# Sinkhorn iterations in three chains, mixing by small diagonals, and Pool's long steps in four pieces

## The reference, cut to what matters

```python
x_norm = x * rsqrt(mean(x * x) + eps)             # x is the normalised sum, 4 streams of C = 256
H_res  = sinkhorn(x_norm @ W_res.T + base)        # 4x4, 50 iterations of row and column normalisation
H_pre, H_post = softmax(x_norm @ W_pre.T + ...), softmax(x_norm @ W_post.T + ...)
H_res  = (1 - g) * I + g * H_res
y      = sum_n(x[n] * H_pre[n]) @ W_branch        # 256
out[i] = sum_j(H_res[i, j] * x[j]) + y * H_post[i]
```

## Time and profile before

| | |
|---|---|
| median of 3 runs | 1298.62 us (1297.89 to 1299.15) |
| the profiled execution | 1296.82 us |
| its span, first to last instruction | 1295.0 us |
| granted clock of PE, mean | 0.916 of 2.4 GHz |
| busy PE, DVE, ACT, POOL | 1070.1, 989.8, 616.4, 546.5 us |
| start of the mixing phase | 1100 us |

### The profile page before, as it was taken

The page is one execution under the profiler, slowest core; times in us unless marked ns, Lnnn a source line. Parts: engine busy times, 40 slices in busy tenths (PEclk is TensorE's granted clock), DMA queues, the critical chain, the costliest instruction groups (busy, mean ns, idle before and its releaser), DMA issues. The chain is left out here.

```text
span 1295.0 us, 24193 instructions
## 1 busy us (share of the span) xinstructions
PE 1070.1 (83%) x8048; PEld 826.3 (64%) x8048; DVE 989.8 (76%) x2908; ACT 616.4 (48%) x1758; POOL 546.5 (42%) x678
## 2 busy tenths in 40 slices
PE   5699999999999999996479999998788874096182
PEld 4477777777877777775356677776566543085071
DVE  6766677766666677765158777787999898999998
ACT  6444455555444455555156776776455542311110
POOL 2523344333333444333137665665454340153194
PEclk9799999999999999998789999999998885597596
DMA  8011101111111101111222232232122111622012
GB/s 362 23 56 40 54 18 55 55 55 55 55 53 41 48 23 55 56 40 40 100 87 76 87 122 85 75 117 86 65 75 70 37 57 41 245 74 89 16 66 97
DMA packets 28652, 95.43 MB, mean 74 GB/s; under 512 B 3760, under 2 KB 7856, under 8 KB 28592
## 3 DMA queue, kind: packets, MB, share of 16 engines
q1 hardware_dynamic: 28592, 94.69, 20.0%
HBM read 64.27 MB, written 27.26 MB: 71 GB/s over the span
## 5 line engine op out<-in xcount | busy, mean ns | idle before, releaser
L614 POOL TENSOR_TENSOR prob_G<-prob_G,rl 128x512 f32<-128x512 f32 x96 | 100.0, 1042 | 258.1 <-DVE rl L502 258.1
L384 ACT ACTIVATE prob_G<-prob_G,negm 128x128 f32<-128x128 f32 x384 | 148.8, 388 | 89.6 <-DVE negm L444 89.6
L245 PE MATMUL ps_qkv<-w_hi,xT_hi 128*128 128x512 f32 x384 | 156.2, 407 | 13.5 <-DVE prob_G L507 8.5
L246 PE MATMUL ps_qkv<-w_lo,xT_hi 128*128 128x512 f32 x384 | 151.4, 394 | 0.0
L247 PE MATMUL ps_qkv<-w_hi,xT_lo 128*128 128x512 f32 x384 | 150.9, 393 | 0.0
L317 PE MATMUL ps_qkv<-wo_hi,aT_hi 128*128 128x512 f32 x256 | 108.0, 422 | 0.0
L319 PE MATMUL ps_qkv<-wo_hi,aT_lo 128*128 128x512 f32 x256 | 102.3, 399 | 0.0
L318 PE MATMUL ps_qkv<-wo_lo,aT_hi 128*128 128x512 f32 x256 | 102.1, 399 | 0.0
L245 PEld LDWEIGHTS ps_qkv<-w_hi,xT_hi 128*128 128x128 f32 x384 | 73.0, 190 | 39.4 <-issue 16.5
L1482 PE MATMUL p_out<-m_xr,m_diag 128*128 128x256 f32 x240 | 58.1, 409 | 46.9 <-POOL m_diag L1649 37.0
L440 DVE TENSOR_TENSOR prob_G<-ps_s,mask 128x512 f32<-128x512 f32 x96 | 65.0, 677 | 41.6 <-PE ps_s L228 41.1
(11 more groups left out here) (218 smaller groups left out, 2987.7 us busy)
## 6 DMA issues: line engine op xcount, KB each, us to landing
rows<-c_row SPq DMA_DIRECT2D x16, 640.0 KB, 3.3
xin<-in_x SPq DMA_DIRECT2D x16, 512.0 KB, 3.3
xres<-in_x SPq DMA_DIRECT2D x16, 512.0 KB, 5.3
x<-xres SPq DMA_DIRECT2D x16, 512.0 KB, 2.6
c_xin<-x SPq DMA_DIRECT2D x16, 512.0 KB, 5.0
c_cin<-in_ctx SPq DMA_DIRECT2D x16, 512.0 KB, 4.3
c_b_xres<-x SPq DMA_DIRECT2D x16, 512.0 KB, 3.2
m_late_row<-rows SPq DMA_DIRECT2D x10, 640.0 KB, 10.9
```

The costliest lines, as they stand in the source:

```text
L245: nc.tensor.matmul(ps_qkv[:, n, :], xT_hi[:, k, :], w_hi[:, k, cols], start=k == 0, stop=False)
L246: nc.tensor.matmul(ps_qkv[:, n, :], xT_hi[:, k, :], w_lo[:, k, cols], start=False, stop=False)
L384: r = nc.scalar.activation(prob(g)[:, j, :], prob(g)[:, j, :], ACT.Exp, bias=negm[:, h:h + 1], accum_out=lsum[:, h:h + 1])
L614: nc.gpsimd.tensor_tensor(prob(g), prob(g), rl[:, g * GROUP:(g + 1) * GROUP].rearrange("p (j o) -> p j o", o=1).to_broadcast([P, GROUP, T] ...
```

## The change: what it does

- **Chains.** There are three, `a` of 5 sequences, `b` of 8, `c` of 3 (`ROWS_OF_CHAINS`). Chain a runs wholly in rounds 6 to 15, 40 steps in each of the rounds 8 to 14, and has more places to be put: behind each product, each pick of weights and each `tq`. Chain b starts in round 14 and has 126 of its steps behind it when the mixing phase begins, c 16. There `weave` lets them take turns, with a few steps of one alone where the other waits for a logarithm; the last steps of c are alone. All is written out, with no loop.
- **Rows.** `rows_x` keeps the normalised features with the lanes regrouped (32 tokens of each of four streams on 128 lanes), `rows_y` the branch. SP issues five DMAs for a row where it issued one.
- **Mixing.** A sequence takes four matmuls over 128 rows and four over 32 rows, 256 columns each, with diagonals of 128x640 in one step: POOL makes them for a and b, DVE for c. For this the coefficients are spread over the lanes: four small matmuls a chain (`sel`), and copies by ACT (for c two by DVE). ACT brings results out in quarters of 256 columns (for c half of them DVE). DVE no longer mixes. The output goes out in four DMAs a sequence.
- **ACT's order** in the mixing phase: copies of a, sequences 0 and 1, the logarithms of b's first block, sequences 2 to 4, those of c's first block and of b's second, copies of b, sequences 5 to 11, the last logarithms of c, sequence 12, copies of c, the last three.
- **POOL's long steps.** From b = 6 the splits (of the sequence two ahead) and the sums run in four pieces of 256 columns. The division of the weights isn't split.
- **Weights.** In rounds 1 to 7 PE transposes them right behind the query's transform rather than behind the key's, and ACT copies them before the key's spectrum.
- The looped rounds are 3 and 4; before they were 3 to 6.

```diff
+ROWS_OF_CHAINS = (5, 8, 3)
+LOOPED = 4
+def weave(dve, *targets):
+    while any(chain.issued < to for chain, to in targets):
+        for chain, to in targets:
+            advance(dve, chain, to, 1)
...
+        for b in range(8, B - 1):
+            if b == 11:
+                parts = {0: at + 3, 1: at + 9, 2: END[0], 3: END[1], 4: END[1] + 10}
+            else:
+                parts = {0: at + 3, 1: at + 9, 2: at + 29, 4: at + 40}
...
+        steps_to[14, 0] += ((one_b, 2),)
+        steps_to[14, 2] += ((one_b, 3),)
+        steps_to[14, 4] += ((one_b, 6),)
+        steps_to.update({(15, 0): ((one_b, 8), (one_a, END[2])), (15, 1): ((one_b, 22),), (15, 2): ((one_a, END[3]), (one_b, 46)), (15, 3): ((one_b, 50),),
+                         (15, 4): ((one_b, 56),), (16, 0): ((one_b, 88),), (16, 3): ((one_c, 2),), (16, 4): ((one_b, 100), (one_c, 6)),
+                         (17, 0): ((one_b, 116),), (17, 4): ((one_b, 126), (one_c, 16))})
+        logs_at = {(6, 1): ((one_a, 1),), (6, 2): ((one_a, 2),), (7, 0): ((one_a, 3),), (7, 1): ((one_a, 4),), (7, 2): ((one_a, 5),),
+                   (11, 2): ((one_a, 6), (one_a, 7), (one_a, 8)),
+                   (14, 1): ((one_b, 1),), (14, 2): ((one_b, 2),), (15, 0): ((one_b, 3), (one_b, 4), (one_b, 5)),
+                   (15, 1): ((one_a, 9), (one_a, 10)), (15, 2): ((one_a, 11),),
+                   (16, 2): ((one_c, 1), (one_c, 2)), (17, 2): ((one_c, 3), (one_c, 4), (one_c, 5))}
...
                     split3(p_a, 0, xn_hi, xn_lo).then_inc(q_ps, 1)
+                    if far and weights_first(b):
+                        transpose_weights()
...
+                chain_logs(b, 0)
+                if far and weights_first(b):
+                    weights_out()
                 if near:
                     key_spectrum(0, f_b)
                     key_spectrum(1, f_c)
...
+            def in_parts(b, dst, a, of, op):
+                width = C if isinstance(b, int) and b >= 6 else D
+                for at in range(0, D, width):
+                    cols = slice(at, at + width)
+                    r = TT(dst[:, cols], a[:, cols], of[:, cols], op)
+                return r
...
+            for chain in chains:
+                pe.wait_ge(coef_step, COEFS * (group(chain) + 1))
+                for g in range(NS):
+                    r = nc.tensor.matmul(p_sel[:, g, 0:chain.n * OWN], sel_sb[:, g, :],
+                                         coef[:, rows, :].rearrange("p b k -> p (b k)"), start=True, stop=True)
+                pe.wait_ge(rows_in[group(chain)], 32 * chain.n)
+                for n in range(chain.first_row, chain.first_row + chain.n):
+                    for g in range(NS):
+                        if 0 < n <= LAST:
+                            pe.wait_ge(out_done, NS * (n - 1) + g + 1)
+                        nc.tensor.matmul(p_out[:, g, 0:C], d[:, g * NS:(g + 1) * NS, :].rearrange("p i t -> p (i t)"),
+                                         xm[n][:, g, :], start=True, stop=False)
+                    for g in range(NS):
+                        lanes = slice(g * W, (g + 1) * W)
+                        nc.tensor.matmul(p_out[:, g, 0:C], d[lanes, N2:N2 + NS, :].rearrange("p i t -> p (i t)"),
+                                         ym[n][lanes, :], start=False, stop=True).then_inc(mix_ps, 1)
...
+            copies(one_a)
+            take_out(0, 2)
+            logs(one_b, FIRST_LOGS + 1, FIRST_LOGS + BLOCK_LOGS)
+            take_out(2, one_a.n)
+            logs(one_c, FIRST_LOGS + 1, FIRST_LOGS + BLOCK_LOGS)
+            logs(one_b, FIRST_LOGS + BLOCK_LOGS + 1, FIRST_LOGS + 2 * BLOCK_LOGS)
+            copies(one_b)
+            take_out(one_b.first_row, LAST - 1)
+            logs(one_c, FIRST_LOGS + BLOCK_LOGS + 1, FIRST_LOGS + 2 * BLOCK_LOGS)
+            take_out(LAST - 1, LAST)
+            copies(one_c)
+            take_out(LAST, B)
```

More of the change, by code:

```diff
@@ L849, in autocorrelation_phase @@
[L849 to L860, removed]
@@ L1095, in body @@
                     key_spectrum(1, f_c)
-                if far:
-                    act.wait_ge(wT_ps, b + 1)
-                    for n in range(2):
-                        nc.scalar.activation(wT[:, n * HALF:(n + 1) * HALF], p_d[:, n, :], ACT.Copy).then_inc(wT_done, 1)
+                if far and not weights_first(b):
+                    weights_out()
                 if ahead:
@@ L1355, in _, with mixing_phase @@
             iterations(pool, body)
-def mixing_phase(nc, rows, facts, early, gate, ident, out):
+def mixing_phase(nc, rows_x, rows_y, facts, chains, gate, sel, fold, out):
     with ExitStack() as ctx:
@@ L1406, in mixing_phase @@
[L1406 to L1427 removed]
+        W = T // NS
@@ new lines, in take_out @@
+            def take_out(first, to):
+                for n in range(first, to):
+                    chain = max((c for c in chains if c.first_row <= n), key=lambda c: c.first_row)
+                    spread_ready(act, chain)
+                    for g in range(NS if n < LAST else 2):
+                        act.wait_ge(mix_ps, NS * n + g + 1)
+                        nc.scalar.activation(ot[n][:, g, :], p_out[:, g, 0:C], ACT.Identity,
+                                             bias=mean[:, n, g:g + 1]).then_inc(out_done, 1)
@@ new lines, in _ @@
+            advance(dve, one_c, one_c.issued + 3)
+            weave(dve, (one_b, BASES[2]), (one_c, one_c.issued + 2))
+            advance(dve, one_c, one_c.issued + 2)
+            coefficients(one_b, lambda: advance(dve, one_c, one_c.issued + 1))
+            advance(dve, one_c, BASES[2])
+            coefficients(one_c, lambda: None)
+            dve.wait_ge(sel_ps, group(one_c) + 1)
+            for j in range(2, NS):
+                dst, src = spread_at(one_c, j)
+                nc.vector.tensor_copy(dst, src).then_inc(spread_by_dve, 1)
@@ new lines, in _ @@
+            spread_ready(dve, one_c)
+            for n in range(LAST, B):
+                folded, own = by_token(n)
+                nc.vector.tensor_tensor(last_diag[n - LAST][:, :, :], folded, own, ALU.mult).then_inc(last_diag_done, 1)
+            for n in range(LAST, B):
+                for g in range(2, NS):
+                    dve.wait_ge(mix_ps, NS * n + g + 1)
+                    nc.vector.tensor_scalar(ot[n][:, g, :], p_out[:, g, 0:C], mean[:, n, g:g + 1], None, ALU.add).then_inc(out_by_dve, 1)
@@ L1680, in _ @@
-            for n in range(EARLY, by_pe.count):
-                diagonals(n, n % 2, False)
-                for j in STREAMS_AFTER.get(n - EARLY, ()):
-                    add_stream(j)
+            pool.wait_ge(const_in, 32)
+            for chain in (one_a, one_b):
+                pool.wait_ge(coef_step, COEFS * (group(chain) + 1))
+                spread_ready(pool, chain)
+                for n in range(chain.first_row, chain.first_row + chain.n):
+                    if n >= 3:
+                        pool.wait_ge(mix_ps, NS * (n - 2))
+                    folded, own = by_token(n)
+                    nc.gpsimd.tensor_tensor(diag[n % 3][:, :, :], folded, own, ALU.mult).then_inc(diag_done, 1)
```

509 lines of the change are left out of this document (207 added, 302 removed).

## The result

The changed kernel takes 1247.56 us (median of 4 runs, 1246.49 to 1251.71) for 1298.88: the ratio is 0.9609, with an interval from 0.9585 to 0.9634. The forecast was 1267 us in a range from 1240 to 1290. The profiled execution has a span of 1245.1 us for 1295.0, 49.9 us less.

The account below looks back on a forecast made before the run. It took PE to set the time before b = 9 and DVE from then on, ending with 66 us of DVE mixing. Terms: 1296.8 - 5 + 5 + 20 - 4 - 46 = 1266.8 us, given as 1267, range 1240 to 1290.

Parts of the forecast that it names:

- first case: Whole kernel: the main forecast of 1267 us, with its own bounds 1250 to 1283 and chance 0.58.
- signs of being wrong: Rounds of 27 or 32 us, mixing before 1110, b's sequences over 3.6 us, or DVE waiting for c's last logarithms.
- Part 1: Rounds 1 to 7: earlier weights remove PE's 0.8 us wait a round; -5 us, bounds 0 and -6.
- Part 2: Rounds 8 to 14: more chain steps, partly offset by smaller port waits and earlier logarithms; +5 us, bounds -8 and +15.
- pieces don't let DVE in: Rival for POOL's long steps: a multiplying step waits for POOL's whole run; +20 us, 1287 us, chance 0.06.
- Part 3: The last three rounds: 159 chain steps instead of 97, and later logarithms; +20 us, bounds +10 and +26.
- first two delays: In the last three rounds: the products start 9.6 us later and the residual comes 12 us later.
- Part 4: Chains in the mixing phase: paired steps, ACT's queue and port waits take 121 us for 124.9; -4 us.
- near tie: Mixing phase: ACT done at 116 us, c needs it at 117; counted as nothing; falling otherwise 1283 us, chance 0.09.
- Part 5: The end, from c's last exponential: 24 us for 70.1; -46 us.
- Steps hide better: Rival in rounds 8 to 14 and mixing: steps cost near 0.1 us, port waits go; 1243 us, chance 0.2.
- Slower: Rival in mixing: matmuls over 32 rows run one by one at half clock, 7.4 us a sequence; 1307 us, chance 0.07.

Follow-up runs that it names:

- key_first: The changed kernel with weights transposed behind the key's transform and copied behind the key's spectrum in every round, as before the change: 1252.87 us, ratio 0.9646.
- exp_early: The changed kernel with chain a's first steps and logarithms moved so no chain exponential heads ACT's round 7: 1246.59 us, ratio 0.9610.
- whole: The changed kernel with POOL's splits and sums undivided in every round: 1275.61 us, ratio 0.9827.
- logs_first: The changed kernel with ACT taking the logarithms of b's first block before the copies of sequences 0 and 1: 1240.88 us, ratio 0.9565.
- diag_pieces: The changed kernel with POOL's 13 diagonals of 128x640 made in four pieces of 160 columns: 1250.28 us, ratio 0.9628.
- in_turns: The changed kernel with each PE matmul over 32 rows directly following the one over 128 rows of its quarter: 1316.75 us, ratio 1.0150.
- old_pieces: The kernel before the change, with only POOL's splits and sums cut into four pieces from b = 7 on: 1286.6 us, ratio 0.9908.

## Why the forecast came out as it did

The sign, the range and the main mechanism held: 66 us of DVE's mixing went, the last rounds and the end took about what was counted, and DVE stayed the bound from b = 8 on. The forecast was 20 us too slow, and the result lies outside its first case's own bounds, 1250 to 1283; the wider range took it in. Three of its signs of being wrong came, each by little: rounds of 27 us (191.0 / 7 = 27.3, where about 30 were expected), a mixing phase from before 1110 (1109.5, expected 1120), and a DVE wait for c's last logarithms (0.45). Parts 1 and 2 left their own bounds in opposite directions, by the +5.2 and -15.6 us of the table, so that the sum came closer than its terms is in part luck. Step by step:

- **Part 1, -5, measured +0.2.** Two steps. The order of the weights gives 3.4 us, not 5 (key_first). And "the chains' Exp and Ln in rounds 6 and 7 cost nothing" failed: ACT's busy share of 16.8 in 23.2 us was taken as cover, but the exponential and its loads stood ahead of what PE and DVE wait for. That cost 3.6 us (rounds 0 to 7 of key_first, 182.7, against 179.1 before); with the exponential moved, round 7 takes 3.9 less (exp_early). The forecast had named 6 us without that cover.
- **Part 2, +5, measured -10.6.** The failing step is the price of a step and of DVE's own waits, not the gain of the pieces. Held steps cost 19.2 us before and 9.4 after, 9.8 less; the forecast said 1.3 a round, 9. It said 0.15 to 0.2 us for each of the 16 steps in new places: DVE's busy time, unchanged in spite of 9.8 us less of holding, gives 9.9 us for 95 more steps, 0.10 each, with the narrower columns in it. And DVE's waits fell by 10.2 us (15.6 to 5.4), where I had counted 3.6. The sum had a slip as well: 6 - 4.6 + 1 is 2.4, and it took 5. So of the 15.6 us some 6.6 are waits, 5.5 the steps (9.9 for 7 x 2.2 = 15.4), 2.6 the slip and 0.7 the holding; the split between waits and steps is arithmetic, no run separates them. The port waits were read from one round, "about 5 us", in a stretch where the mean was 19.2 / 7 = 2.7; that the arrangement with its 283 steps would cost 33 us of holding without pieces (whole) wasn't seen, and the rival "pieces don't let DVE in", priced at 20 us, would have been 28.
- **Part 3, +20, measured +21.2.** The first two delays held within 0.7 us. The third was 4.5 us for 1, of which DVE's wait for PE is 3.0, and the last 4.0 for 7: two misses that offset one another. The forecast's list also places only 139 of its 159 steps; by the trace 37, 26, 42 and 54 lie in the four pieces. No run tests these delays.
- **Part 4, -4, measured -9.5.** b's first logarithms: 9.07 us for 11. Later logarithms: nothing for 4. c's last and its exponential 1.9 for 2.4. Held steps: 9.0 us for 5, at 1.26 us for a diagonal as estimated; nearly each of them caught a step. The steps themselves 95.5 for 98.6: a pair took 0.36 us for 0.345 (12 steps in 2.17), and c alone 0.253 for 0.285 (six in 1.52). Chain b alone, in the last rounds, takes the same 0.36 a step (six in 2.16, from 1080.80 us), so c's steps cost nothing in a pair, as the forecast had it.
- **The near tie** came out within 0.45 us in the profiled execution and fell the other way in those of exp_early and logs_first, with waits of 3.4 us each. The forecast counted it as nothing and priced the fall at 16; it was 3, because only the first two sequences of b's group ran at half clock. Together with b's wait, in the same queue of ACT, it swallowed the gains of diag_pieces and exp_early.
- **Part 5, -46, measured -49.9.** The second of the last three sequences ran at the full clock: 11.5 us for the three where 13.6 were counted. What stands ahead of them took 3.6 us (1224.90 to 1228.50) for 5.35.
- **The rivals.** *Steps hide better* was nearest in its total, 1243, and right about the seven rounds (195 us, measured 191), but wrong in the rest: the logarithms did not come early. *Slower*, matmuls over 32 rows one by one at half clock, was priced at 7.4 us a sequence and +40; in_turns made that case real, at 9.2 us and +69.

## What to carry to other kernels

Where a short step of one engine shares a port with long steps of another, cut the long ones that it really meets: a step waits for the rest of what runs, so here a quarter of the length was a quarter of the price, and with half as many steps again it was worth 28 us for 11. A share of busy time is no cover for an instruction at the head of a round; look at what stands behind it in its queue. When an edit gains what it should in its stretch and the total doesn't move, look for the wait that grew, remove it, and try the edit again before it is thrown away: the shorter diagonals and the earlier exponential gave 4.3 and 2.4 us only once the queue was mended.

## What the runs showed of the hardware

- A multiplying step of DVE with both inputs in SBUF that meets a long instruction of POOL ends about 0.1 us after it (2.20 us for a step of 0.24). The Trainium skill, SBUF — State Buffer, Who interferes with whom, says that a DVE instruction with two SBUF inputs contends with a GpSimd instruction that reads SBUF, over a pair of ports that is an exclusive lock; the rows agree, and whole puts 24 us on it. Between pieces the step does get in: the 32 held steps of the changed kernel's rounds lose 0.29 us each, the 15 of old_pieces 0.46, three of them at the undivided division.
- POOL's short instructions on 128x1 hold nothing that the traces show: in whole a step at 945.29 us takes 0.24 us with 0.49 us of such a one still to run. Why isn't tested.
- Cutting costs POOL time: four pieces of 128x256 take 2.8 us from first start to last end (0.73 each, overlapping a little) for 2.4 undivided, and a diagonal in four 1.7 for 1.26.
- Four matmuls over 32 rows side by side take 0.71 us at the full clock. Each change between 32 and 128 rows costs about 0.30 us at the half clock. At the full clock it is 0.20: in the changed kernel at 1206 us the passes next to a change start 0.31 and 0.32 us apart for 0.22.
- In in_turns the granted clock stayed at 0.50 for the whole phase, with PE busy in 30.0 of 30 us from 1230 on. That was not expected, and its cause is open. The Trainium skill, TensorE: Matmul & The Clock Gate, Part 1, says that activity releases the throttle, which this run does not show for such a mixture.
- The matmuls of b's group found their clock risen after one sequence in the changed kernel and after two in exp_early, logs_first and diag_pieces, and DVE's last wait for ACT was 3 us longer in the first two of these. That the spread of a kernel's own runs, 5 us for the changed one, comes from this isn't shown; its slowest run has the lowest mean clock (0.911 for 0.915 to 0.917), and so has that of diag_pieces (0.908 for 0.912 to 0.918).
